# Expert rows of a routed feed-forward placed and scattered in two token halves, in groups of 32 rows

## What is computed

```
z      = layernorm(x2)                  # 1024 tokens
logits = z @ gate_weight.T              # 16 experts
top 2 experts of each token, softmax over the two
h[e]   = mean over the tokens routed to expert e of silu(z @ w1[e].T)      # 512 wide
y[e]   = h[e] @ w2[e].T                 # 128 wide
out    = x2 + sum over the two experts of weight * y[e]
```

## Time and profile before

| | us |
|---|---|
| median of 3 runs (lowest to highest) | 303.64 (301.27 to 304.04) |
| the profiled execution | 302.46 |
| its span on the chip | 300.3 |
| PE, DVE, ACT, POOL busy in the span | 232.3, 196.6, 173.4, 50.1 |
| mean granted TensorE clock | 0.903 |

### The profile page before, as it was taken

The page is one execution under the profiler, slowest core; times in us unless marked ns, Lnnn a source line. Parts: engine busy times, 40 slices in busy tenths (PEclk is TensorE's granted clock), DMA queues, the critical chain, the costliest instruction groups (busy, mean ns, idle before and its releaser), DMA issues.

```text
span 300.3 us, 7194 instructions
## 1 busy us (share of the span) xinstructions
PE 232.3 (77%) x2811; PEld 160.7 (53%) x2811; DVE 196.6 (65%) x424; ACT 173.4 (58%) x253; POOL 50.1 (17%) x64
## 2 busy tenths in 40 slices
PE   0999389999999988699997788888681200899985
PEld 0689046766767666479895466655470200333253
DVE  5648788999999999643459766787578700354012
ACT  8578979989899890483436655665642100245420
POOL 7005939400000000100020000000001774000000
PEclk9999759999999999969999889999975555799999
DMA  6910000000000004900000000000291111600002
GB/s 147 386 46 2 1 0 2 0 2 0 0 0 0 0 0 157 398 8 0 3 0 0 2 0 2 0 3 0 98 419 45 52 45 59 194 2 0 2 0 72
DMA packets 8819, 16.14 MB, mean 54 GB/s; under 512 B 736, under 2 KB 5088, under 8 KB 8416
## 3 DMA queue, kind: packets, MB, share of 16 engines
q1 hardware_dynamic: 8288, 14.83, 14.0%
q0 software_dynamic: 512, 1.05, 0.9%
HBM read 12.73 MB, written 3.15 MB: 53 GB/s over the span
## 4 chain that ended last, share of the span: by engine, by line
PE 64%; DVE 9%; ACT 9%; issue 7%; POOL 5%; DMA 3%; SPq 1%; POOLq 0%; DVEq 0%; ACTq 0%
PE ps L1236 11%; PE ps L1220 8%; PE ps L1523 7%; POOL slot_rows L479 5%; PE ps L1335 3%; ACT arena L563 3%; PE ps L1386 3%; PE ps L1303 2%; DVE t_k L946 2%; PE ps L1536 2%; PE ps L1347 2%; PE ps L1124 2%; PE ps L1293 2%; DMA r_sb<-in_rows 2%; PE ps L1290 1%
## 5 line engine op out<-in xcount | busy, mean ns | idle before, releaser
L563 ACT ACTIVATE arena<-ps,one_less_sq 128x1024 bf16<-128x1024 f32 x64 | 68.7, 1113 | 7.8 <-PE ps L1220 7.7
L1236 PEld LDWEIGHTS ps<-arena 128*128 128x128 bf16 x1536 | 47.8, 97 | 19.9 <-issue 7.9
L1236 PE MATMUL ps<-arena 128*128 (+1 forms) x1536 | 50.6, 184 | 2.2 <-ACT arena L563 2.1
L1220 PE MATMUL ps<-wide,sel 128*128 (+1 forms) x128 | 40.1, 397 | 7.7 <-ACT arena L563 5.6
L905 DVE TENSOR_REDUCE msda<-wide 128x768 f32 x32 | 45.2, 1457 | 0.0
L900 DVE TENSOR_TENSOR wide<-ps,wide 128x768 f32<-128x768 f32 x32 | 29.8, 953 | 4.6 <-PE ps L1236 4.6
L479 POOL DMA_INDIRECT slot_rows<-nrm,slots x16 | 16.5, 1032 | 78.4 <-DVE slots L1042 73.8
L713 ACT ACTIVATE sel<-ps 128x512 f32<-128x512 f32 x12 | 7.2, 597 | 29.0 <-PE ps L1526 29.0
L1523 PE MATMUL ps<-arena,w_sb 128*64 x48 | 22.4, 611 | 0.0
L1526 PE MATMUL ps<-late,w_sb 128*64 128x512 f32 x48 | 22.4, 611 | 0.0
L946 DVE TENSOR_REDUCE t_k<-ps 128x2 f32<-128x512 f32 x32 | 20.6, 685 | 0.4 <-PE ps L1347 0.3
(11 more groups left out here) (282 smaller groups left out, 471.0 us busy)
## 6 DMA issues: line engine op xcount, KB each, us to landing
arena<-in_w_t SPq DMA_DIRECT2D x1, 4096.0 KB, 14.4
wide<-in_w_t SPq DMA_DIRECT2D x1, 2048.0 KB, 7.6
slot_rows<-t_c SPq DMA_DIRECT2D x1, 1536.0 KB, 11.7
wide<-in_w_t SPq DMA_DIRECT2D x1, 1536.0 KB, 11.3
late<-slot_rows SPq DMA_DIRECT2D x6, 256.0 KB, 4.9
w_sb<-in_weights SPq DMA_DIRECT2D x1, 1480.0 KB, 8.9
x_sb<-in_x SPq DMA_DIRECT2D x4, 128.0 KB, 2.1
wide<-in_w_t SPq DMA_DIRECT2D x1, 512.0 KB, 8.4
```

What stands on the lines that cost most here:

```text
L563: nc.scalar.activation(hot[:, u, 2 * c:2 * c + 2, :, :], ps[:, 2 * (c % 2):2 * (c % 2) + 2, :].rearrange("r p (b q) -> r p b q", b=B), ACT ...
L1220: ins = nc.tensor.matmul(ps[:, 2 * (c % 2) + p % 2, :], sel[:, bass.ds(i % 4, 1), p, :].rearrange("k h j -> k (h j)"), terms_t[:, bass.ds( ...
L1236: ins = nc.tensor.matmul(ps[:, 4 + b, p * NK * DH:(p + 1) * NK * DH], hot[:, u, p, b, :], rhs, start=(s == 0), stop=(s == PARTS - 1))
```

## The change

**Constants.** `GRAIN` is 32 instead of 64, and slots are numbered in each token half by itself: 1024 rows and their padding fit into 12 tiles a half (`HALF_TILES`), so there are 24 tiles as before, the first 12 for tokens of half 0. Each tile has four grains. There are two DRAM buffers, one for each half, each zeroed by its own DMA.

**Placing.** The gate's work is cut into `gate(h)` and `rank(h)` on PE, `choose(h)`, `place(h)`, `experts_of(h)` and `slot_experts(h)` on DVE, and half 0 gets its slots before half 1 is chosen. The turn of half 0's norm stands ahead of `project_out(1)` on PE, ACT's copy of x2 for half 0 ahead of half 1's standard deviation, and the Sqrt table is loaded at the end of `unit_step(8)`.

**Scatter.** POOL waits for the slots of each half and scatters 8 DMAs for each; SP waits for half 0's eight and reloads 3 groups, then for half 1's.

**Expert tiles.** Of a tile's four grains PE multiplies the first with the weights where they lie and the other three with copies. DVE makes 72 copies instead of 24, 16 buffers ahead at most, the first 12 (four tiles) before the routing weights. Register loads are of 4 values, one a group on PE and three a group on DVE. ACT copies the columns out, no longer DVE.

**Attention.** In PE's `unit_step`, `project(k+1, 0)` stands ahead of `weigh_values`, and `scores(k, 1)` ahead of `turn_out`, of the turn of `lna` and of `project(k+1, 1)`. In ACT's, the high part of the queries stands ahead of `unit_out`.

The diff, cut to its core (renamed constants and shapes are left out):

```diff
-GRAIN = 64
-COLS = 32
-SLOT_TILES = (T * TOPK + E * (GRAIN - 1)) // P + 1
+GRAIN = 32
+HALF_TILES = (HALF * TOPK + E * (GRAIN - 1)) // P + 1
+SLOT_TILES = 2 * HALF_TILES
+HALF_GROUPS = HALF_TILES // GROUP
+STAGED = QUADS - 1
...
@@ SP
-            for c in range(TOPK):
-                sp.wait_ge(scattered[c], 16 * TILES)
-
             sp.wait_ge(st_mm, UH * UNITS)
             for g in range(SLOT_GROUPS):
+                h, n = g // HALF_GROUPS, g % HALF_GROUPS
+                if n == 0:
+                    sp.wait_ge(scattered[h], 16 * 4 * TOPK)
...
@@ POOL
             for t in range(TILES):
+                h = t // 4
+                if t % 4 == 0:
+                    pool.wait_ge(slots_ready, h + 1)
                 for c in range(TOPK):
...
@@ ACT, unit_step
+                if k + 1 < UNITS:
+                    high_parts(k + 1, 0)
                 if k >= 2:
                     unit_out(k - 2)
-                if k + 1 < UNITS:
-                    high_parts(k + 1, 0)
...
+                if k == UNITS:
+                    nc.scalar.activation(table_junk[:, :], eps_c[:, :], ACT.Sqrt)
...
             ln_out(lns["lnf"], 2, z2, halves=(0,))
+            x2_out(0)
             ln_std_of(lns["lnf"], (1,))
             ln_out(lns["lnf"], 2, z2, halves=(1,))
+            x2_out(1)
...
+            columns_out(0)
+            columns_out(1)
+            for g in range(SLOT_GROUPS):
+                for t in range(GROUP * g, GROUP * g + GROUP):
+                    act.wait_ge(h_mm, t + 1)
+                    if t >= len(hidden_at):
+                        act.wait_ge(sum_mm, (t - len(hidden_at)) // GROUP + 1)
+                    nc.scalar.activation(hidden_at[t % len(hidden_at)], ps[:, 2 + t % 4, :], ACT.Silu).then_inc(h_ready, 1)
+                if g + 2 < SLOT_GROUPS:
+                    columns_out(g + 2)
...
@@ DVE
+            def stage(tiles):
+
+                for n in range(STAGED * tiles.start, STAGED * tiles.stop):
+                    t, q = n // STAGED, n % STAGED
+                    if n >= len(staged_at):
+                        dve.wait_ge(h_mm, (n - len(staged_at)) // STAGED + 1)
+                    if q == 0 and t % GROUP == 0:
+                        h, g = t // HALF_TILES, t % HALF_TILES
+                        dve.wait_ge(experts_ready, h + 1)
+                        at = [nc.values_load_multi_w_load_instructions(
+                            expert_at[GRAIN * r:GRAIN * r + 1, h, g:g + GROUP], [mybir.EngineType.DVE], min_val=0, max_val=E - 1,
...
+                              for r in range(1, QUADS)]
+                    nc.vector.tensor_copy(staged_at[n % len(staged_at)], w1_sb[:, bass.ds(at[q][t % GROUP], 1), :].rearrange(
+                        "d e f -> d (e f)")).then_inc(staged, 1)
+
             ln_apply(lns["lnf"], x2_k, (0,))
             residual_stats(1)
+            choose(0)
             ln_apply(lns["lnf"], x2_k, (1,))
...
+            place(0)
+            experts_of(0)
+            choose(1)
+            place(1)
+            dve.wait_ge(ld_w1, 16)
+            dve.wait_ge(x2_mm, TILES)
+            stage(range(0, GROUP))
...
+            slot_experts(0)
+            experts_of(1)
+            slot_experts(1)
...
+            stage(range(GROUP, SLOT_TILES))
...
@@ PE, unit_step
                 if k < UNITS:
                     scores(k, 0)
+                if k + 1 < UNITS:
+                    project(k + 1, 0)
                 if k >= 2:
                     weigh_values(k - 2)
-                if k + 1 < UNITS:
-                    project(k + 1, 0)
                 if k >= 1 and k - 1 < UNITS:
                     scores_t(k - 1, 0)
+                if k < UNITS:
+                    scores(k, 1)
                 if k >= 2:
                     turn_out(k - 2)
                 if k == 0:
                     turn(lns["lna"], 4, (1,))
                 if k + 1 < UNITS:
                     project(k + 1, 1)
-                if k < UNITS:
-                    scores(k, 1)
...
             turn_outputs(1)
+            turn(lns["lnf"], 2, (0,))
             project_out(1)
...
+            gate(0)
             pe.wait_ge(late_consts, 1)
+            rank(0)
+            turn(lns["lnf"], 2, (1,))
+            gate(1)
+            rank(1)
...
@@ PE, expert_tiles
                     nc.tensor.matmul(ps[0:GRAIN, 2 + t % 4, :], x_cols[:, t * P:t * P + GRAIN],
-                                     w1_sb[:, bass.ds(at[t], 1), :].rearrange("d e f -> d (e f)"))
-                    pe.wait_ge(staged, t + 1)
-                    nc.tensor.matmul(ps[GRAIN:P, 2 + t % 4, :], x_cols[:, t * P + GRAIN:t * P + P],
-                                     staged_at[t % len(staged_at)]).then_inc(h_mm, 1)
+                                     w1_sb[:, bass.ds(at[j], 1), :].rearrange("d e f -> d (e f)"))
+                    for q in range(1, QUADS):
+                        entry = STAGED * t + q - 1
+                        pe.wait_ge(staged, entry + 1)
+                        ins = nc.tensor.matmul(ps[GRAIN * q:GRAIN * (q + 1), 2 + t % 4, :],
+                                               x_cols[:, t * P + GRAIN * q:t * P + GRAIN * (q + 1)],
+                                               staged_at[entry % len(staged_at)])
+                    ins.then_inc(h_mm, 1)
```

More of the change, by code:

```diff
@@ L34 @@
 SPLIT = 3 * AD
-VCOLS = 32
+VGRAIN = 32
 PAIRS = AH // 2
@@ L1036, in _ @@
-            link(nc.vector.tensor_reduce(first_slot[:, :], quads_before[:, :, :], AX_X, ALU.add))
-            link(nc.vector.tensor_tensor(slot_of[:, :, :], ranks[:, 0:TILES, :],
-                                         first_slot[:, :].unsqueeze(1).to_broadcast([P, TILES, E]), ALU.add))
-            link(nc.vector.tensor_tensor(picked_slot[:, :, :, :], picked[:, :, :, :],
-                                         slot_of[:, :, :].unsqueeze(1).to_broadcast([P, TOPK, TILES, E]), ALU.mult))
-            with nc.allow_low_precision(reason="slot numbers are whole and below 2560"):
-                nc.vector.tensor_reduce(slots[:, :, :], picked_slot[:, :, :, :], AX_X, ALU.add).then_inc(slots_ready, 1)
@@ new lines, in place @@
+            def place(h):
+                tiles = slice(4 * h, 4 * h + 4)
+                dve.wait_ge(rank_mm, h + 1)
+                link(nc.vector.tensor_scalar(quads_e[:, h, :], ranks(h)[:, 4, :], 1.0 / GRAIN, ROUND, ALU.mult, ALU.add))
+                link(nc.vector.scalar_tensor_tensor(out=quads_before[:, :, :],
+                                                    in0=quads_e[:, h, :].unsqueeze(1).to_broadcast([P, E, E]),
+                                                    scalar=-ROUND, in1=before32[:, :, :], op0=ALU.add, op1=ALU.mult))
+                link(nc.vector.tensor_reduce(first_slot[:, h, :], quads_before[:, :, :], AX_X, ALU.add))
+                link(nc.vector.tensor_tensor(slot_of[:, :, :], ranks(h)[:, 0:4, :],
+                                             first_slot[:, h, :].unsqueeze(1).to_broadcast([P, 4, E]), ALU.add))
+                link(nc.vector.tensor_tensor(picked_slot[:, :, :, :], picked[:, :, tiles, :],
+                                             slot_of[:, :, :].unsqueeze(1).to_broadcast([P, TOPK, 4, E]), ALU.mult))
+                with nc.allow_low_precision(reason="slot numbers are whole and below 1536"):
+                    nc.vector.tensor_reduce(slots[:, :, tiles], picked_slot[:, :, :, :], AX_X, ALU.add).then_inc(slots_ready, 1)
```

204 lines of the change are left out of this document (94 added, 110 removed).

## The result

| | before | after |
|---|---|---|
| median of the runs (lowest to highest), us | 303.22 (301.27 to 304.04) | 284.62 (284.51 to 284.63) |
| the profiled execution | 302.46 | 284.63 |
| its span | 300.3 | 282.8 |
| PE, DVE, ACT, POOL busy | 232.3, 196.6, 173.4, 50.1 | 228.8, 210.1, 177.7, 50.0 |
| mean granted clock | 0.903 | 0.932 |

The ratio is 0.939, with a 95% interval of 0.934 to 0.945. One execution of the changed kernel (293.27 us, at a granted clock of 0.887) fell in the slower state of the chip and is left out.

What follows compares the result with a forecast made beforehand. POOL's sixteen scatters between slots and first transpose were taken as the bound. From 302.46: attention +1.1, earlier slots -3.9, eight fewer scatters -10.1, wait for half 1 +0.6 gave 290.2, put at 291 toward the median; range 287.5 to 297.5.

Steps and rivals of the forecast that it cites:

- Eight fewer in front: Scatter: eight instead of sixteen scatters stand before half 0's reload, -10.1 us.
- The forecast wait: Expert stage: PE's group 3 waits for half 1's reload, 0 to 0.8 us, taken as +0.6.
- Step 0 +2.0: Attention step 0: the turn and project(1,1) queue behind scores(0,1), which waits for the first maxima, +2.0 us.
- unit 1 +0.0: Attention unit 1: the first exponentials, behind a table load, set the end either way, 0.
- rivals A and B: Expert stage: register loads make DVE the bound, moderately (294.6, or 295.5 from the median; 0.18) or fully (313.7; 0.08).
- 19.7 + 18x: Expert stage: DVE's last copy ends 19.8 + 18x us after the first transpose, x being one register load; bound past 0.53.
- Rival D: Scatters: weight copies lock GpSimd out, delaying both halves; 298.7 us at most, chance 0.05.
- 0.22 less a unit: Attention units 2 to 6: the new order, laid on old durations, saves 0.22 us each, -1.1 together.
- the clock counted as a risk only: Attention: a longer half-speed dip of PE's clock could add up to 2 us.
- the attention term: Attention order as a whole, step 0 to unit 7: +1.1 us.
- Rival C: Attention: the new order costs 2 to 3 us more than counted, through the clock or ACT; 293 us, chance 0.11.
- From the last unit to the first scatter: Last attention unit to slots: half 0 is placed earlier, first scatter at 227.4 instead of 231.24, -3.9 us.

Runs made afterwards that it cites:

- a_onewait: Changed kernel, but SP waits for the scatters of both halves before its first reload: 295.97 us (two runs), ratio 0.977.
- after_again: The changed kernel run again as it is: 283.97 us, ratio 0.944.
- after_5: The changed kernel once more as it is, in a later measurement: 284.57 us, ratio 0.940.
- a_proj: Changed kernel with project(k+1,0) and ACT's order as changed, but scores(k,1) back in its old place: 287.79 us, ratio 0.951.
- a_scores: Changed kernel with only scores(k,1) moved, from unit 1 on; project(k+1,0), ACT's order and step 0 as before: 283.43 us, ratio 0.937.
- a_step0: Changed kernel with the old order in attention step 0 alone: 284.25 us.
- a_step0_5: Changed kernel with the old order in attention step 0 alone, again in more rounds: 284.87 us, ratio 0.939.
- a_warm: Changed kernel with the old order in step 0 and six needless matmuls on PE ahead of its wait for the route: 283.65 us, ratio 0.939.
- aw_new: Changed kernel, new order in every step, with six needless matmuls on PE ahead of its wait for the route: 285.88 us, ratio 0.945.
- a_warm_5: Changed kernel with the old order in step 0 and six needless matmuls on PE, again in more rounds: 284.54 us, ratio 0.943.

## Why the prediction was wrong, and where it was right

**Right.** What bound the kernel: the scatters between the slots and the first transpose. Eight fewer in front: the first transposes came 14.4 after the first scatter (15.1 forecast), and the turns of group 3 at 26.2 (26.1 forecast). a_onewait shows that the mechanism is this one. That the second figure came out to 0.1 is luck: PE started 0.7 early, had no wait for half 1 where 0.6 was put, and took 11.8 us for three groups instead of 10.3, as it stood at 0.50 for 5.8 us there and for some 3 in before. The forecast wait shows in after_again and after_5 instead (0.82 and 1.11), whose turns came at 25.3 and 25.7. Step 0 +2.0 and unit 1 +0.0 came out to a tenth. Placing a half took the 2.0 that were worked out, and the first scatter followed the slots by 0.86. PE never waited for DVE's copies; rivals A and B did not happen. (DVE's free time and five groups add up to 19.7 + 18x, not 19.8, and rival A's 295.5 should be 295.8 from the median; neither touches the forecast.)

**Rival D, and the rule weighed against the rows.** Beside copies the scatters came every 1.39 us (231.73 to 235.89), with single steps from 1.26 to 1.43, against 1.26 without: the row of before, not a full lock, held. The sum went by the row and was right there.

**Wrong, step 1: "0.22 less a unit".** It measured 0.47 in units 3 to 6. The new order was laid out on the old durations, and the 0.55 from normalization to maxima was kept as DVE's own time. In before, though, the maxima (189.19) stood behind two things that ended in the same 0.05 us, scores(k,1) and the normalization:

```profile
188.66 0.50 PE L1347 MATMUL ps<-xm 64*128 64x256 f32 x4
...
188.87 0.29 DVE L965 TENSOR_TENSOR msda<-ps,inv_sum 128x128 f32<-128x128 f32 x1
```

Free of the first, they follow the start of the normalization at 0.45 (186.31, 186.76). The turned outputs also came 0.14 earlier than my rounded sum of PE's pieces. a_proj and a_scores show the two limits apart. Over units 2 to 6 this is 1.2 us.

**Wrong, step 2: the clock counted as a risk only.** The earlier trace rows showed half speed in unit 2, and I asked only whether it might get longer. It vanished: unit 2 lasts 2.00 less, of which 0.47 is the order and some 1.5 the clock. a_step0 and a_step0_5, the same kernel, show that 1.5 by themselves: unit 2 takes 6.20 without the stretch and 7.72 with it. The two steps together, less 0.3 for unit 7, whose +0.5 was taken as +0.2, are the 2.5 us by which the attention term missed. Rival C had the right cause and the wrong direction; no case stood below the forecast for it.

**Undersized: from the last unit to the first scatter,** -4.5 for -3.9. The gate of half 0 was through 11.2 after the turned maxima of unit 7, not 11.5, and `place(0)` began at 15.7, not 16.3. No run undoes this placing by itself; its 4.5 is read from the two traces. From group 3 to the last sums 0.9 went that was set at 0: a group of four tiles takes 5.01 (250.09 to 255.10), not the 5.17 of the earlier trace rows. I had put a tile with four 32-column products at equal or dearer and taken 0. No run shows whether the form of the products or DVE's column copies, which are gone, make the difference.

**Not the change's.** 1.5 before the attention starts, and 0.3 around and behind it, are differences between two executions. Adding 0.8 toward the median was wrong as well: in later measurements the median of before was 302.3 to 302.8, the profiled execution's own time. So the 6.4 us to the forecast are 2.5 of attention, 0.6 up to the first scatter, 0.9 of the expert stage, 1.8 that are not the change's and the 0.8, less 0.1 for the scatters. My range went 3.5 below the forecast, while all but one of these came out fast together.

## What to carry to other kernels

Where one engine's row of equal steps stands between two stages, release the next stage by halves; then look for the new meeting point, here the sixteenth scatter against three groups of PE work, since ahead of it neither a faster PE nor fewer loads gave anything that these runs can tell. When a new order is laid on old durations, find every wait that ends within a tenth of the one removed, and count the gain only when all are moved: here each half alone gave -0.14 to +0.12 us a unit and both together 0.46. A stretch at half clock on the path can go as well as come; give both signs a price. A forecast of one stage can be met by errors that cancel, so compare its parts too.

## What the runs showed of the hardware that I had not expected

- In the median a register load from SBUF took 0.33 (TensorE) and 0.56 us (VectorE) for 4 values, 1.07 for 12 and 1.87 for 24. The Trainium skill, "DMA: Bandwidth & Descriptors", "Latency and other measured facts", gives about 600 ns as the floor; the medians here for 4 values lie below it.
- Much of such loads disappears under queued copies: 18 more loads of 0.56, 10 us in all, moved DVE's last copy by 3.3 and the last sums by 0.2 to 1.0, by which record of the changed kernel it is set against.
- Moving two groups of matmuls within a step of PE made a stretch of 3.3 to 6.8 us at 1.2 GHz vanish from all eight records with the new order, several us behind the first place where the order differs; with one step's order moved back it stood in two records of five. Where the kernel is the same, it cost 1.5 us.
- The sixteenth indirect scatter landed 2.34 us after its start in one record and 3.77 in another, and the end of the kernel moved with it.
- Six needless matmuls held PE at 2.4 GHz through the next idle stretches in one record (a_warm) and not in two others (aw_new, a_warm_5), where the two idle stretches behind them made 3.5 and 3.0 us instead of 2.7.
